# A two-layer transformer kernel: setup moved into the main program, first batch loaded first, rows fetched by two queues

## The chip, the cores and the metric

The kernel runs on one core of a Trainium2 chip. A core has TensorE (matmuls), VectorE (DVE in the rows), ScalarE (ACT), GpSimd (POOL) and SyncE (SP), each with its own list of instructions; they meet at semaphores. SP and ACT also issue DMA transfers, each in its own queue. The metric is the device time of one execution in microseconds, lower is better.

## What is computed

Four batches of 1024 tokens with 128 features pass four blocks, each with a layer norm ahead and a residual sum behind:

```python
x = x + attention0(layernorm(x))   # 16 heads of 8, causal, W_qkv and W_out
x = x + circulant(layernorm(x))    # fft, 128x128 product, ifft, bias
x = x + attention1(layernorm(x))   # 16 heads, one 8x8 weight for all heads, Wu and bu
x = x + experts(layernorm(x))      # 8 experts, top 2 by softmax of a small gate
```

## The kernel before

**Three programs, one after the other.** `setup` (lines 348 to 442) loads and prepares, `pipeline` (474 to 1042) does both attention layers and the circulant block, `experts` (1045 to 1174) the last block. Each is a block of instructions for all engines, and the engines wait for one another at its end.

**setup.** SP loads constants, weights and then all of x (2 MB, line 364), and raises every later semaphore by one, which is why waits of the pipeline are written `past(count)`, one more than the count. ScalarE's queue loads small weights. GpSimd clears buffers, among them the part of `k_rows` that is constant (line 388). VectorE repeats the 8x8 weights (`w8r`, 399), casts constants (401, 402) and moves transposed or multiplied weights out of PSUM (405 to 420), which TensorE makes (428 to 442).

**pipeline.** Attention is done in groups of four heads: 4 batches x 4 groups x 2 layers = 32 groups. What each engine does, and in which sequence, comes from one list, `ORDER`, that all engines walk. It is written out by hand in the strings `LINES`: a letter takes the next item of its stream.

- `r`: one of 18 "score" fills of a group: matmuls of queries and keys in a split bf16 form (line 602), two PSUM banks each, whose row maxima VectorE takes (930). These banks are a ring of two pairs.
- `H`: the "shift": the maxima are turned and written by DMA into rows of `q_rows` (549), so that the next matmuls subtract them.
- `u`: one of 36 "units" of a group: the scores again, transposed and shifted (634), then Exp on ScalarE (748) and for some the causal mask on GpSimd (857). A line of the strings holds the 36 units of one group, but for the first line, which has none.
- `v`, `c`, `O`: product with the values (657), its copy out of PSUM (767), its transpose and division (620, 978, 980).
- `w`: the DMA loads of a group's `q_rows` and `k_rows` (`load_rows`, nine transfers for each of two row tiles).
- `x`: the steps between, in the order of `steps_between`: for each batch the layer norm (`stats` 1001 to 1013, `rstd` 490 to 501, `norm` 1029), transposes `turn` (667), projections (677, 680), splitting of q and k into three bf16 parts, and their `store` in DRAM (521), from which `load_rows` reads. The first batch is split by ScalarE and VectorE (`part`, 810, 814, 1037, 1041), later ones by GpSimd (`split`, 896 to 905).

Layer norms ahead of layer 0 are on VectorE, most others on GpSimd. Transposes, projections and units share three PSUM banks in turn, and each is moved out by ScalarE (`evacuate`, 748), so a fourth waits until the first has been moved. The batch 0 stores of the first group's heads come first, on SP, then rows 0, then the stores of the other heads (538).

Of the kernel before, what the change touches and what calls it, by code (L numbers as in the profile page):

```python
# [93 lines left out]
def masks_before(n, pb):  # L94
# [23 lines left out]
    "uvruvuruuvcruuruvOuruuvruvuruuvcruuruvruuuvruruuuvruuuruvuuHuurruvuruw",  # L118
    "uvruvuruuvcruuruvOuruurxuvruvuruxruvcruuurvruuvruruuuvuruxxuuuvuHuruvuuuwrrvvx",
    "uruuvcruuuruOuruuvrurxuuvvruuuvcruxurxvruuvruruxxuruuvruxxuuuHvuruuuvuruuwrvvx",  # L120
    "uruuvcruuruOuuruvrxuruuvuruvruuxvcrxuruvruxxruuvruruxruuurvuxHuuvrxuruxxuruvruuxrxuw",
    "urvuvruruxxruurvcxrxuuOuuruvruuvxxruvruuuvcxrxruuuvurxuvHuuuvruruuuvruuruuruvuruw",
    "uruvuruuvruuruvcuruurvuOuruuvvruxruuruvcruxuruvHuuuvruruvuruuvruuurvuruuwr",
    "uuvruuvruuvcruuruvOuruuvvruuuvcruruuvruruuvuruuxxuuuvuHuruvuuurvuruuwr",
# [12 lines left out]
    "uruvuvruuruvcruuuxxuuuvuHuOuuuvxvruruuvcuruurxvuruvurxuuvruruxruuurvruuvruw",  # L137
    "uxruvruvuruuvcruuruvOuruuvuruvuruvcuuHuvruruvuruuuvruruuuvruruuurvuruuwr",
    "uuvuruvruuvcruuurvOuruuvruxuruvuruvcxHuuvruruvuruuuvruruuuvruruuurvuruuwr",
    "uuvuruvruuvcruuurvOuruuvruuxxuuuvuvcHuruuvxruuvruuuvrxuruuvruuuruuruvxruwr",  # L140
    "uxuvruvuruxruvcruuurvuOuruuvruuvruuuvcruruuvHuvruruuvruuuruvruuuruvruruuw",
    "uruvuvruuruvcuruurvuOuruuvruuvruuuvcruruuvHuvruruuvruuuruvruuuruvruruuw",
    "uruvuvruuruvcuruurvuOuruuvruxruuuvruvcruxuvHruuruvruuvruuuruvruruuurvuruuwr",
# [10 lines left out]
def preparation(layer, b):  # L154
# [7 lines left out]
    steps = normalisation(2 * layer, b) + [("bias", 2, b)] * layer  # L162
    (q0, q1), (k0, k1), (v0, v1) = halves(0), halves(1), halves(2)
# [184 lines left out]
def setup(nc, m, dram, sem, phase_semaphores):  # L348
    ident = m.const[:, C_ID:C_COS]
    cos, sin, nsin = (m.const[:, c:c + P] for c in (C_COS, C_SIN, C_NSIN))  # L350
    loaded, head_loaded, repeated, made, used, half, ready = (
        sem(n) for n in ("setup_loaded", "setup_w8_loaded", "setup_w8_repeated", "setup_psum", "setup_evacuated",
                         "setup_half", "setup_ready"))
    x_loaded, own = sem("setup_x_loaded"), sem("setup_memset")
    with nc.Block() as block:
        @block.sync
        def _(sp):
            sp.dma_start(m.const[:, :], dram["consts"]).then_inc(loaded, 16)
            sp.dma_start(m.raw[:, 0:3, :], dram["L0_attn_W_qkv"].rearrange("(n o) c -> o n c", o=P)).then_inc(loaded, 16)
            sp.dma_start(m.raw[:, 3, :], dram["L0_attn_W_out"]).then_inc(loaded, 16)  # L360
            sp.dma_start(m.raw[:, 4, :], dram["L1_attn_Wu"]).then_inc(loaded, 16)
            sp.dma_start(m.raw[:, 5, :], dram["L0_ffn_w_freq_real"]).then_inc(loaded, 16)
            sp.dma_start(m.raw[:, 6, :], dram["L0_ffn_w_freq_imag"]).then_inc(loaded, 16)
            sp.dma_start(m.x[:, :, :], dram["L0_attn_x"].rearrange("b (t p) d -> p (b t) d", p=P)).then_inc(x_loaded, 16)

            for semaphore in phase_semaphores:
                sp.sem_inc(semaphore, 1)
            sp.wait_ge(x_loaded, 16)

        @block.scalar  # L370
        def _(act):
            for n, name in enumerate(("L1_attn_Wq", "L1_attn_Wk", "L1_attn_Wv")):
                act.dma_start(m.w8[:, n, :], dram[name]).then_inc(head_loaded, 16)
            act.dma_start(m.bias_ffn[:, :], dram["L0_ffn_bias"].rearrange("(a d) -> a d", a=1).broadcast_to([P, D])).then_inc(m.late_loaded, 16)
            act.dma_start(m.bias_u[:, :], dram["L1_attn_bu"].rearrange("(a d) -> a d", a=1).broadcast_to([P, D])).then_inc(m.late_loaded, 16)
            act.dma_start(m.wg1[:, :], dram["L1_ffn_wg1"]).then_inc(m.late_loaded, 16)
            act.dma_start(m.bg1[:, :], dram["L1_ffn_bg1"].rearrange("(g a) -> g a", a=1)).then_inc(m.late_loaded, 16)
            act.dma_start(m.wg2[:, :], dram["L1_ffn_wg2"]).then_inc(m.late_loaded, 16)

        @block.gpsimd  # L380
        def _(pool):
            nc.gpsimd.memset(m.vg[:, :, :, :, :], 0.0).then_inc(own, 1)
# [42 lines left out]
        def _(pe):  # L425
            pe.wait_ge(loaded, 6 * 16)
            for n in range(4):
                last = nc.tensor.transpose(m.psum[:, 0, n * P:(n + 1) * P], m.raw[:, n, :], ident)
# [801 lines left out]
```

## Time and profile before

| | |
|---|---|
| median of 3 runs | 1220.77 us (1218.82 to 1221.8) |
| the profiled execution | 1220.89 us, span 1219.2 us |
| mean granted TensorE clock | 0.969 |
| TensorE busy | 1132.4 us (93%) |
| VectorE busy | 901.7 us (74%) |
| ScalarE busy | 770.1 us (63%) |
| GpSimd busy | 401.4 us (33%) |

The span runs from the first to the last instruction of the profile; the time of the execution is 1.7 us longer. Busy time of TensorE is modelled, and matmuls overlap. A granted clock of 1.00 is 2.4 GHz, one of 0.50 is 1.2 GHz, and a number between is a mean over time at either.

### The profile page before, as it was taken

The numbers are of one execution on the slowest core, as the hardware profiler recorded it, in microseconds if no ns is written. First come the engines' busy times: TensorE is split into PE (matmuls) and PEld (weight loads), VectorE is DVE, ScalarE is ACT, GpSimd is POOL, SyncE is SP. The second block draws the span as 40 slices with busy tenths as digits, with TensorE's granted clock in tenths as the row PEclk, the third lists the DMA queues.
The fourth block names the chain that finished last, engine by engine and source line by source line (L and its number), as shares of the span: only waits on it lengthen the run. The fifth ranks groups of instructions, "written<-read, shape, count | busy, mean of one in ns | idle before, by whom it ended". The sixth has DMA issues, their size and how long they took to land. (4 is left out here: it accounts for less than half of the span.)

```text
span 1219.2 us, 26837 instructions
## 1 busy us (share of the span) xinstructions
PE 1132.4 (93%) x9927; PEld 542.5 (44%) x9927; DVE 901.7 (74%) x1461; ACT 770.1 (63%) x1397; POOL 401.4 (33%) x667
## 2 busy tenths in 40 slices
PE   3479999999999999999999999999999799999997
PEld 2224343444344344433444344433342357777776
DVE  4698889998998999898899998898892253223223
ACT  1327678777888778787777787777777542322322
POOL 3143452555226462555356452142252000000000
PEclk9669999999999999899999999999998989999999
DMA  3230420112111011002111210011100000000000
GB/s 108 94 115 28 123 79 29 28 28 73 53 29 35 28 54 53 28 29 66 53 37 34 79 29 28 27 34 47 30 3 2 1 1 1 17 0 17 0 18 18
DMA packets 35336, 47.35 MB, mean 39 GB/s; under 512 B 8848, under 2 KB 15120, under 8 KB 35216
## 3 DMA queue, kind: packets, MB, share of 16 engines
q1 hardware_dynamic: 34640, 45.61, 13.1%
q8 instruction: 74, 1.21, 0.4%
q10 hardware_dynamic: 576, 0.15, 0.1%
q14 instruction: 46, 0.38, 0.1%
HBM read 30.53 MB, written 14.68 MB: 37 GB/s over the span
## 5 line engine op out<-in xcount | busy, mean ns | idle before, releaser
L748 ACT ACTIVATE probs<-psum 128x512 f32<-128x512 f32 x1152 | 614.3, 604 | 199.8 <-PE psum L634 197.6
L930 DVE TENSOR_REDUCE block_max<-psum 128x8 f32<-128x1024 f32 x576 | 672.3, 1218 | 70.4 <-PE psum L602 67.0
L634 PE MATMUL psum<-q_rows,k_rows 50*128 50x512 bf16 (+3 forms) x1536 | 325.1, 330 | 14.4 <-ACT probs L748 10.9
L657 PE MATMUL psum<-probs,vg 128*32 128x512 f32 (+3 forms) x3072 | 329.0, 504 | 7.4 <-POOL probs L857 4.4
L857 POOL TENSOR_SCALAR_AFFINE_SELECT probs<-probs 128x512 f32<-128x512 f32 (+1 forms) x320 | 173.9, 547 | 448.0 <-ACT probs L748 444.4
L602 PE MATMUL psum<-k_rows,q_rows 48*128 48x128 bf16 (+2 forms) x2560 | 261.4, 266 | 27.8 <-DMA k_rows<-k_split 17.7
L602 PEld LDWEIGHTS psum<-k_rows,q_rows 48*128 48x128 bf16 x2560 | 114.7, 95 | 180.6 <-DVE block_max L930 74.9
L634 PEld LDWEIGHTS psum<-q_rows,k_rows 50*128 50x128 bf16 x1536 | 105.1, 94 | 166.0 <-ACT probs L748 124.0
L1162 DVE SCALAR_TENSOR_TENSOR x<-psum,probs,x 128x128 f32 x256 | 69.1, 343 | 144.4 <-PE psum L1080 144.0
L1102 ACT ACTIVATE probs<-psum 128x1024 f32<-128x1024 f32 x64 | 65.5, 1024 | 151.5 <-PE psum L1067 151.5
L1080 PEld LDWEIGHTS psum<-w_out,probs 128*128 128x128 f32 x1024 | 119.2, 192 | 14.8 <-issue 12.9
L1080 PE MATMUL psum<-w_out,probs 128*128 128x128 f32 x1024 | 119.3, 275 | 0.0
L1067 PE MATMUL psum<-v,w_in 128*128 (+1 forms) x256 | 116.8, 600 | 0.6 <-PEq L504 0.6
L657 PEld LDWEIGHTS psum<-probs,vg 128*32 128x32 f32 x3072 | 63.0, 108 | 111.2 <-issue 70.1
L599 PE MATMUL psum<-mask 64*128 64x256 bf16 (+1 forms) x512 | 72.9, 334 | 0.8 <-DVE block_max L930 0.5
L875 POOL TENSOR_SCALAR xn<-x,mv,rstd 128x128 f32<-128x128 f32 x88 | 69.2, 798 | 0.3
L1067 PEld LDWEIGHTS psum<-v,w_in 128*128 128x128 f32 x256 | 46.9, 193 | 48.1 <-issue 47.9
L978 DVE RECIPROCAL rden<-psum 128x32 f32<-128x32 f32 x32 | 11.4, 357 | 53.1 <-PE psum L620 52.7
L599 PEld LDWEIGHTS psum<-mask 64*128 64x128 bf16 x512 | 20.5, 95 | 45.5 <-DVE block_max L930 24.1
L767 ACT ACTIVATE out_t<-psum 128x512 f32<-128x512 f32 x64 | 39.1, 611 | 0.1
L677 PE MATMUL psum<-xn_t,w 128*128 128x512 f32 x64 | 36.9, 668 | 0.3 <-ACT probs L748 0.2
L620 PE MATMUL psum<-const,out_t 128*128 128x128 f32 x256 | 34.9, 279 | 2.1 <-DVE block_max L930 1.2
(107 smaller groups left out, 617.4 us busy)
## 6 DMA issues: line engine op xcount, KB each, us to landing
k_rows<-k_split SPq DMA_DIRECT2D x384, 32.0 KB
q_rows<-q_split SPq DMA_DIRECT2D x64, 96.0 KB
q_split<-parts SPq DMA_DIRECT2D x21, 256.0 KB
k_split<-parts SPq DMA_DIRECT2D x21, 256.0 KB
q_rows<-q_split SPq DMA_DIRECT2D x64, 64.0 KB
q_rows<-q_split SPq DMA_DIRECT2D x64, 32.0 KB
out<-x SPq DMA_DIRECT2D x4, 512.0 KB, 3.2
q_rows<-shift_t SPq DMA_DIRECT2D x64, 8.0 KB
```

The costliest lines, as they stand in the source:

```text
L599: nc.tensor.matmul(blocks[:, :, upper], m.mask[tile, j, :], m.mask[tile, 2 + j, upper].unsqueeze(1).broadcast_to([ROW_TILE, 4, P - ROW_TIL ...
L602: done = nc.tensor.matmul(m.psum[:, bank, col:col + w], m.q_rows[rows_of(e, False), buf, pair, i * P:(i + 1) * P], m.k_rows[rows_of(e, Fal ...
L634: done = nc.tensor.matmul(m.psum[:, bank, col:col + w], m.k_rows[rows_of(e, True), buf, pair, kb * P:(kb + 1) * P], m.q_rows[rows_of(e, Tr ...
L657: done = nc.tensor.matmul(m.psum[32 * hh:32 * hh + 32, OUT_BANK, q0 % BANK:q0 % BANK + w], m.vg[:, n % 2, kb, hh, :], m.probs[:, (n * len( ...
L748: nc.scalar.activation(out, m.psum[rows, UNIT_AT[number % UNIT_DEPTH], 0:columns], function, **more).then_inc(bank_read, 1)
L857: nc.gpsimd.affine_select(out=tiles, in_=tiles, compare_op=ALU.is_ge, fill=0.0, base=0, pattern=pattern, channel_multiplier=-1).then_inc(m ...
L875: done = nc.gpsimd.tensor_scalar(m.xn[:, t, :], m.x[:, n, :], m.mv[:, n, 0:1], m.rstd[:, n:n + 1], ALU.subtract, ALU.mult)
L930: nc.vector.tensor_reduce(out, blocks, axis=AX.X, op=ALU.max).then_inc(ring_read, 1)
L1067: last = nc.tensor.matmul(m.psum[:, 2 * j + half, :], m.w_in[:, e % E, j * P:(j + 1) * P], m.xn_t_all[:, b + e // E, half * BANK:(half + 1 ...
L1080: last = nc.tensor.matmul(m.psum[:, bank + t // 4, (t % 4) * P:(t % 4 + 1) * P], m.hidden[:, 2 * (e % 2) + j, t * P:(t + 1) * P], m.w_out[ ...
L1102: nc.scalar.activation(m.hidden[:, 2 * (e % 2) + j, :], m.psum[:, 2 * j:2 * j + 2, :].rearrange("p a b -> p (a b)"), ACT.Gelu).then_inc(ge ...
L1162: last = nc.vector.scalar_tensor_tensor(xt[:, b, t, :], m.psum[:, bank + t // 4, (t % 4) * P:(t % 4 + 1) * P], top[:, b, t, e:e + 1], xt[: ...
```

## The change

`setup` is gone; its instructions stand at the heads or in the middle of the pipeline's instruction lists, without the wait of all engines between. x is loaded in two transfers, batch 0 ahead of everything else. The first weights go through PSUM bank 3 and a ScalarE copy, the others later through banks 4 to 6. Statistics and reciprocal deviations of batch 1 come before batch 0 is transposed, those of batch 2 before batch 1 is. Stores and row loads of batch 0's keys and of the second row tile move to ScalarE's queue. `LINES` is rewritten for the first groups and in many places behind (shown: the first four; 19 of the 33 lines are as some line of before, most of them at another place).

```diff
 LINES = (
-    "xxxxxxxxxxxxxxxxxxxxwwwxxxxxxrrxxxrxxrxxrxxrxxrxxxxxxxrrrrrrrrrrrrrHrrr",
-    "uuuruxxxxuruuruvuuuvvuuuvcuuuvuxuuvruruxuruvuruxruurvuruxruuvrxuruuxuwrvrvxxHvcrrxxxO",
-    "uurxrxuuruuruuvruxxruuvuvruuruvcxuruxurvurxxxxxuuvuururuvuuuuvuuuuvuuxuwvvrxrvrxcHxOxrxxr",
-    "uuuruxruxuruvruuruxruurxvuvruxxrxxuruvcuuruvxrxuuvrurxuuuvururuuvuHuuurruvuruw",
...
+    "xxxxxxxxxxxxxxxxxxxxxxwwwxxxxxxxxxxxxxxxxxrxxxxxxxrrrrrrrrrrrrrrrrrrrHrrr",
+    "uuuruxxuruuruvuuxvuvruruxuvcruuruvruxruurvuruxrxuruxxuruvHuxxruruvuruxxruuvruruxxruwr",
+    "uuvuruvruuvcruuurvuOuruuxxvvruuuvcxrurxuuvruuxxxxxuvururuvuuuuvuuuuvuuuwxvvvHxcrrxO",
+    "uruxruuruuruvxururuxruuvxuvruruxxuruvcurxxruuvruruxxxxxuxrurvuuuvxHuurruvuruuvruuuwr",
...
     steps = normalisation(2 * layer, b) + [("bias", 2, b)] * layer
+    if (layer, b) == (0, 0):
+        steps[4:4] = normalisation(0, 1)[:2]
+    elif layer == 0 and b < 3:
+        steps = steps[2:]
+        if b == 1:
+            steps[2:2] = normalisation(0, 2)[:2]
...
-def load_rows(m, engine, n, rows_loaded):
+def load_rows(m, engine, n, rows_loaded, tiles=(0, 1)):
...
-    for e in (0, 1):
+    for e in tiles:
...
+def first_stores(m, engine, which, heads, done):
+    dest = (m.q_dram, m.k_dram)[which][0].rearrange("h r d (b t) -> r b h d t", b=B)
+    for part in range(PARTS):
+        engine.dma_start(dest[part, 0, heads], m.parts[heads.start * DH:heads.stop * DH, which, part, :]).then_inc(done, 16)
...
         @block.sync
         def _(sp):
+            x = dram["L0_attn_x"].rearrange("b (t p) d -> p (b t) d", p=P)
+            sp.dma_start(m.x[:, 0:TT, :], x[:, 0:TT, :]).then_inc(m.x_first, 16)
+            sp.dma_start(m.const[:, :], dram["consts"]).then_inc(m.loaded, 16)
+            sp.dma_start(m.raw[:, 0:3, :], dram["L0_attn_W_qkv"].rearrange("(n o) c -> o n c", o=P)).then_inc(m.loaded, 16)
+            for semaphore in sems + m.later:
+                sp.sem_inc(semaphore, 1)
+            for n, name in ((3, "L0_attn_W_out"), (4, "L1_attn_Wu"), (5, "L0_ffn_w_freq_real"), (6, "L0_ffn_w_freq_imag")):
+                sp.dma_start(m.raw[:, n, :], dram[name]).then_inc(m.raw_loaded, 16)
+            sp.dma_start(m.x[:, TT:NT, :], x[:, TT:NT, :]).then_inc(m.x_rest, 16)
...
+                        if which == 0:
+
+                            sp.wait_ge(cast_made, past(3))
+                            sp.wait_ge(rest_made, past(3))
+                            first_stores(m, sp, 0, slice(0, GH), first_stored)
+                        continue
...
+                        sp.wait_ge(m.own, 5)
+                        load_rows(m, sp, 0, rows_loaded, (0,))
+                        first_stores(m, sp, 0, slice(GH, HEADS), stored)
...
+            first_weights()
             for item in ORDER:
...
                     project(item)
+                    if item[1:] == (0, 0, 2, 1):
+                        further_weights()
...
+            act.wait_ge(m.made, 1)
+            nc.scalar.activation(m.w[:, Q0:V0 + 1, :].rearrange("p a b -> p (a b)"), m.psum[:, OUT_BANK, 0:3 * P], ACT.Copy).then_inc(m.used, 1)
...
+                elif item == ("store", 0, 0, 1):
+
+                    act.wait_ge(cast_made, past(4))
+                    act.wait_ge(rest_made, past(4))
+                    first_stores(m, act, 1, slice(0, GH), first_stored)
+                elif item == ("rows", 0):
+
+                    act.wait_ge(first_stored, past(STORES))
+                    act.wait_ge(m.own, 5)
+                    load_rows(m, act, 0, rows_loaded, (1,))
+                    first_stores(m, act, 1, slice(GH, HEADS), stored)
...
+            def constants_cast():
+
+                dve.wait_ge(m.loaded, 2 * 16)
+                nc.vector.tensor_copy(m.ident_bf[:, :], ident).then_inc(m.cast, 1)
+                nc.vector.tensor_copy(m.mask[:, :, :].rearrange("p a b -> p (a b)"), m.const[:, C_MASK:C_HEAD]).then_inc(m.cast, 1)
+                dve.wait_ge(m.head_loaded, 3 * 16)
+                for n in range(3):
+                    nc.vector.tensor_copy(m.w8r[:, n, :, :], m.w8[:, n, :].unsqueeze(1).broadcast_to([DH, HEADS, DH])).then_inc(m.repeated, 1)
...
-                    if s > 0:
+                    if s == 0:
+
+                        dve.wait_ge(m.x_first if b == 0 else m.x_rest, 16)
+                    else:
...
                     done.then_inc(normalised, 1)
+                    if (s, b, half) == (0, 0, 1):
+                        constants_cast()
...
+                        if which == 1:
+                            further_weights()
```

`further_weights` on TensorE holds the three small matmuls, two transposes and six matmuls that setup had for the other weights, and on VectorE the seven moves out of PSUM. It stands behind the last projection of batch 0 on TensorE and behind the last part of batch 0's keys on VectorE.

## Rows read from the trace of the kernel before

**Rows 1.** Stages: busy us of each engine, granted TensorE clock, DMA share, GB/s.

```profile
17.70:50.30 32.60, 8.24 (x34) 5.21 (x34) 18.69 (x84) 9.85 (x13) 0.00 (x0) 0.76 0.12 38
82.00:145.00 63.00, 59.73 (x525) 23.32 (x526) 56.53 (x124) 45.60 (x87) 24.13 (x30) 0.94 0.30 84
145.00:900.00 755.00, 732.91 (x7344) 303.90 (x7347) 679.16 (x884) 584.42 (x1115) 333.04 (x579) 0.99 0.15 41
```

**Rows 2.** DMA issues of the start: size, us from issue to landing.

```profile
const<-in_consts SPq DMA_DIRECT2D x1, 552.0 KB, 3.8
...
x<-in_L_attn_x SPq DMA_DIRECT2D x1, 0.5 KB, 13.1
```

**Rows 3.** Timeline of the first 26 us: start, duration, instruction, [idle before].

```profile
3.03 0.45 ACTq L376 DMA_DIRECT2D wg<-in_L_ffn_wg  x1
3.13 7.10 POOL L388 MEMSET k_rows<- 32x4096 f32 x2
...
3.84 0.93 SPq L364 DMA_DIRECT2D x<-in_L_attn_x  x1
...
10.67 0.42 DVE L402 CAST mask<-const 128x512 bf16<-128x512 f32 x1
...
17.75 1.65 DVE L1001 BATCH_NORM_STATS2 stats<-x 128x6 f32<-128x128 f32 x8 [0.53 <-PEq L355]
...
20.10 0.17 DVE L1011 TENSOR_SCALAR newton<-mv 128x8 f32<-128x8 f32 x1
...
23.23 2.14 DVE L1029 TENSOR_SCALAR xn<-x,mv,rstd 128x128 f32<-128x128 f32 x8
```

**Rows 4.** Line 399 alone: shortest, median and longest of three, in ns.

```profile
L399 DVE COPY w8r<-w x3: 1407/1482/3606, 5.2 to 6.7; 8x128 f32<-8x128 f32 x3
```

**Rows 5.** Timeline around 87 us.

```profile
87.26 0.64 POOL L857 TENSOR_SCALAR_AFFINE_SELECT probs<-probs 128x512 f32<-128x512 f32 x1 [0.83 <-ACT probs L748]
87.34 0.58 DVE L490 TENSOR_SCALAR newton<-newton 128x8 f32<-128x8 f32 x1
```

**Rows 6.** Timeline from 26 to 54 us.

```profile
26.33 4.52 PE L677 MATMUL psum<-xn_t,w 128*128 128x512 f32 x8
...
32.46 2.36 DVE L1037 TENSOR_TENSOR qk<-qk,parts 128x1024 f32<-128x1024 f32 x2 [7.09 <-ACT parts L810]
...
34.81 2.36 DVE L1041 TENSOR_TENSOR parts<-qk,parts 128x1024 bf16<-128x1024 f32 x2
35.82 1.07 ACT L748 ACTIVATE v<-psum 128x512 f32<-128x512 f32 x2
...
38.35 1.84 SPq L521 DMA_DIRECT2D k_split<-parts  x3
...
42.22 1.10 SPq L467 DMA_DIRECT2D q_rows<-q_split  x3
...
46.50 2.00 SPq L471 DMA_DIRECT2D k_rows<-k_split  x6
...
50.29 1.03 PE L602 MATMUL psum<-k_rows,q_rows 48*128 48x512 bf16 x4 [17.66 <-DMA k_rows<-k_split]
...
51.41 2.29 SPq L538 DMA_DIRECT2D k_split<-parts  x3
...
53.13 2.08 PE L677 MATMUL psum<-xn_t,w 128*128 128x512 f32 x2
```

**Rows 7.** Two stretches behind the idle time, columns as in rows 1.

```profile
50.30:55.50 5.20, 5.20 (x16) 2.30 (x16) 2.35 (x2) 1.40 (x3) 0.00 (x0) 0.50 0.66 209
55.50:63.00 7.50, 7.50 (x56) 3.93 (x56) 6.13 (x5) 3.38 (x6) 5.29 (x4) 1.00 0.34 105
```

**Rows 8.** Timeline from 63 to 82 us.

```profile
63.01 10.28 DVE L930 TENSOR_REDUCE block_max<-psum 128x8 f32<-128x1024 f32 x9 [0.52 <-PE psum L602]
...
75.90 0.42 DVE L938 TENSOR_REDUCE low<-block_max 128x32 f32<-128x256 f32 x1
...
81.94 1.03 PE L634 MATMUL psum<-q_rows,k_rows 50*128 50x512 bf16 x3 [0.32 <-DMA q_rows<-shift_t]
```

More of the change, by code:

```diff
@@ L463, in load_rows @@
                     for d in (m.q_dram[layer], m.k_dram[layer]))
-    for e in (0, 1):
+    for e in tiles:
         for first, count in ((0, 3), (3, 2), (5, 1)):
@@ L511, in _ @@
                     if (layer, b) == (0, 0):
[L513 to L517 removed]
+                        if which == 0:
[3 more added lines that the diff above has]
+                        continue
+                    sp.wait_ge(split_done, past(at_split(layer, b, which) + 1))
                     dest = (m.q_dram, m.k_dram)[which][layer].rearrange("h r d (b t) -> r b h d t", b=B)
[L519 removed]
                     for part in range(PARTS):
[L521 removed]
+                        sp.dma_start(dest[part, b], m.parts[:, which, part, :]).then_inc(stored, 16)
                 elif kind == "rows":
@@ L532, in _ @@
                         sp.wait_ge(bank_filled, past(UNIT_AT_ORDER["unit", n - GROUPS, NU - 1] + 1))
-                    load_rows(m, sp, n, rows_loaded)
                     if n == 0:
-                        for which, dram_parts in enumerate((m.q_dram[0], m.k_dram[0])):
-                            dest = dram_parts.rearrange("h r d (b t) -> r b h d t", b=B)
-                            for part in range(PARTS):
-                                sp.dma_start(dest[part, 0, GH:HEADS], m.parts[GH * DH:P, which, part, :]).then_inc(stored, 16)
+                        sp.wait_ge(m.own, 5)
+                        load_rows(m, sp, 0, rows_loaded, (0,))
+                        first_stores(m, sp, 0, slice(GH, HEADS), stored)
+                    else:
+                        load_rows(m, sp, n, rows_loaded)
                     if n == GROUPS:
@@ L581, in scores @@
                 buf = n % GROUPS
+                if (n, s) == (0, 0):
+                    pe.wait_ge(m.cast, 2)
                 if s == 0:
@@ L825, in _ @@
         def _(pool):
+            nc.gpsimd.memset(m.vg[:, :, :, :, :], 0.0).then_inc(m.own, 1)
+            nc.gpsimd.memset(m.block_max[:, :, :, :, :, :, :].rearrange("p n h e a i k -> p (n h e a i k)"), -3.0e38).then_inc(m.own, 1)
+            k_words = m.k_rows[:, :, :, :].rearrange("p g h t -> p (g h t)").bitcast(FP32)
+            pool.wait_ge(m.own, 2)
+            for e in (0, 1):
+                nc.gpsimd.memset(k_words[ROW_TILE * e + 32:ROW_TILE * (e + 1), :], TWO_ONES).then_inc(m.own, 1)
+            pool.wait_ge(m.own, 4)
+            nc.gpsimd.memset(m.vg[:, :, :, :, DH:DH + 1], 1.0).then_inc(m.own, 1)
+            pool.wait_ge(m.own, 5)
             v = m.v[:, :, :].rearrange("p (b t) (g h d) -> p b g t h d", b=B, g=GROUPS, h=GH)
@@ L958, in _ @@
                 if kind == "score":
+                    if item[1:] == (0, 0):
+                        dve.wait_ge(m.own, 5)
                     take_scores(item, bank)
@@ L1186, in preln_two_layers @@
         moe = [sem(f"moe_{name}") for name in EXPERT_SEMAPHORES]
-        setup(nc, m, dram, sem, flow + moe)
+        m.later = moe
+        m.x_first = sem("setup_x_first")
+        m.x_rest = sem("setup_x_rest")
+        m.loaded = sem("setup_loaded")
+        m.raw_loaded = sem("setup_raw_loaded")
+        m.head_loaded = sem("setup_head_loaded")
+        m.repeated = sem("setup_repeated")
+        m.made = sem("setup_made")
+        m.used = sem("setup_used")
+        m.cast = sem("setup_cast")
+        m.own = sem("setup_own")
         pipeline(nc, m, dram, flow)
```

155 lines of the change are left out of this document (57 added, 98 removed).

## The prediction

> **What bounds the kernel now.** I read the whole span by stages first [rows 1], then the start instruction by instruction. From 145 to 900 us TensorE is busy 732.9 of 755 us at granted clock 0.99, VectorE 679, ScalarE 584: in the long middle TensorE sets the pace, and 22.1 us of it are idle. From 82 to 145 TensorE is busy 59.7 of 63, so here too little is lost but clock (0.94). From 17.7 to 50.3 it is busy 8.2 of 32.6 us. So the run is a start in which TensorE waits, then a stretch that it fills. Whatever brings its first "unit" matmul (81.94 us [rows 8]) forward should come off the end, as long as the stretch behind it keeps its length.
>
> What fills the start: x lands 13.1 us after its issue at 3.84, so at 16.94 [rows 2, 3]. The barrier ends and statistics begin at 17.75, normalising at 23.23 and ends 25.37 [rows 3]. Projections and splitting end at 37.17, stores are issued until 40.19, the loads of group 0's rows start at 42.22, and the first score matmul starts at 50.29 [rows 6]. Eighteen score reductions of VectorE later group 0's maxima are reduced at 75.90, and the first unit follows at 81.94 [rows 8].
>
> **The change, part by part.** All times are of the profiled execution.
>
> *x first, no barrier.* The first batch of x is now first in SP's queue: 512 KB. The nearest row is the 552 KB of constants, first in the queue before: issued at 0.80, landed 3.8 us later, at 4.6 [rows 2]. x has shorter pieces, so I take 5.2 (bounds 4.6 and 7.5, twice the time). Statistics and aggregation took 20.10 - 17.75 = 2.35 us, so the first small TENSOR_SCALAR comes due at 7.55.
>
> *GpSimd in the way.* The memsets stay at the start; the two of k_rows run from 3.13 to 10.23 [rows 3]. Before, VectorE was waiting for the weights meanwhile. What it did then was the copies of w8r, and these took 1.41, 1.48 and 3.61 us [rows 4] for 8 x 128 elements, the last ending at 10.3, just after the memset, although a cast of 128 x 512 takes 0.42 [rows 3]. Later a TENSOR_SCALAR of 128 x 8 at 87.34 took 0.58 us, against 0.17 for one like it [rows 3], and ended at 87.92, when the GpSimd operation of 87.26 to 87.90 did [rows 5]. So the chain of TENSOR_SCALARs will be held until 10.23. The Trainium skill says this as a rule, on the page "SBUF — State Buffer", section "Who interferes with whom": a VectorE copy or tensor_scalar in a two-port mode and a GpSimd instruction lock one port pair against each other, and the later one waits for the whole of the earlier. It speaks against this change, since it takes back part of the early load; the two rows agree with it. From 10.23, the rest of the chain as before (25.37 - 20.10 = 5.27) ends the normalising at 15.5; without the hold it would be 5.2 + 7.62 = 12.8.
>
> *Constants and the weights.* The constants and W_qkv now queue behind 512 KB. If that delays them by as much as 552 KB took in all, they land at 4.6 + 3.8 = 8.4; with three transposes and one ScalarE copy they are ready by about 11. The first projection came 26.33 - 25.37 = 0.96 after the normalising [rows 3, 6], so it comes at 16.5. They cost nothing; if later than that they push everything by the excess. Behind the normalising VectorE casts the constants and repeats w8: 0.42 for the larger cast, some 1.3 us in all (estimate from that row, five copies).
>
> *Statistics of batch 1 brought forward.* VectorE must now finish them before the splitting (parts). They wait for the other 1.5 MB of x. SP issues that after 36 semaphore increments, which no row prices, and four weights, at some 0.45 each if like the small load on ScalarE's queue [rows 3]. Before, all bytes had landed at 16.94; the order of bytes changes, not their sum. I take 16 (bounds 14.5 and 18.5). After the casts VectorE is free at 16.8, statistics and reciprocal take 23.23 - 17.75 = 5.48, to 22.3. The parts could start 32.46 - 25.37 = 7.09 after the normalising, at 22.6. So this move is just hidden; x landing at 18.5 costs 1.4. The parts end 4.71 later [rows 6]: **27.3** instead of 37.17 (bounds 26.2 without the hold and 28.7).
>
> *Stores and rows by two queues.* K's three stores move to ScalarE's queue, 1.84 us from 27.4; the rows start 42.22 - 40.19 = 2.03 after them, at 31.3. Of 18 row loads (42.22 to 48.5, 0.35 each) ScalarE issues nine, 3.1 us, then three more stores, 2.29 [rows 6]: it is held until **36.7**. ScalarE's own issues cost 0.45 where shown [rows 3], like SP's. The rows land at 31.3 + 3.1 + 1.8 = 36.2. On SP the remaining Q stores shorten alike, and rows 1 and 2 come earlier than before; they are needed only some 20 us later.
>
> *What is queued behind.* In the new order all of batch 1's transposes and projections but the last stand before the first score on TensorE, and their evacuations, with those of V of batch 0, stand on ScalarE behind its DMA issues. So the rows are not what the first score waits for. From 36.7: two V evacuations and one of the transposes at 0.54 [rows 6], 38.3; then q0, q1, k0, k1, v0. One 128 x 512 projection takes 1.13 at clock 1.00 (4.52 for four) and 2.08 after an idle stretch [rows 6]; from 50.30 the clock was 0.50 for 5.2 us of steady work and then 1.00 [rows 7]. So two at 2.08 and three at 1.1: first score at **45.8** (43.8 all fast, 48.7 all slow).
>
> *Other weights.* VectorE's seven operations lay between 10.67 and 17.75 before [rows 3], so they and TensorE's between them take 7.1 us at most, until 34.4 now; batch 1's normalising (2.14) ends by 36.5 and batch 2's statistics by 42. All this is covered by the same wait; beyond 36.7 the normalising would delay the transposes one for one.
>
> *Scores.* Before, projections stood between the first seven scores: the seventh ended at 63.01. From there eleven took 12.89, or 1.17 each. Eighteen now take 21.1, 0.5 is what VectorE waits for the first of them (as before 63.01), and some 0.8 goes to the one projection left in between (part of 1.1 to 2.08): 45.8 + 22.4 = 68.2 [rows 8], and the first unit comes 81.94 - 75.90 = 6.04 later: **74.2**, against 81.94. Gain 7.7 us, bounds 3.4 (x late by 1.4, low clock 2.9) and 10.8 (no hold 1.1, high clock 2.0).
>
> *The order behind.* The same matmuls are there, so I charge only idle time. From 82 to 145 TensorE idled 3.3 us [rows 1], mostly where a group's shift came last in its line. The new line puts shift 1 before twelve units of group 0, and VectorE no longer has batch 2's statistics there. I take 1.5 gained; bounds 3.3 gained and 3.3 lost. From 145 on the lines are rearranged, and without a trace of them I take nothing, bounds a few us either way.
>
> **Sum:** 7.7 + 1.5 = 9.2. The profiled execution took 1220.89 us (span 1219.2), 0.1 above the median 1220.77: 1220.9 - 9.2 = **1211.7**.
>
> **Rivals.**
>
> *VectorE's lead counts, not TensorE's.* VectorE is 56.5 of 63 us busy behind the start [rows 1], and TensorE's idle moments there may all be its waits. The seventh score then ends at 45.8 + 0.8 + 0.5 + 8.2 = 55.3 against 63.01, and 5.48 of statistics lie before it: 13 ahead, 1208. Against it: TensorE is busier in that stretch.
>
> *ScalarE's issues eat the gain.* Fifteen DMA issues now hold ScalarE on the chain. If each costs 0.6 us more there than on SP, the 9.2 are gone and the time is 1221, no change. The rows of small issues speak against it; none shows a store or a row load on that queue.
>
> *The new order stalls in the middle (slower).* One mechanism: scores run further ahead of the units there, so TensorE more often waits at a full ring or for an evacuation. Idle there is 22.1 us now. It eats the gain when it grows by 9.2 us, and the kernel is slower beyond +0.3% when it grows by 13. If it doubled, 1220.9 - 9.2 + 22.1 = 1233.8. For it: TensorE is at 97% and any misplaced wait counts. Against it: 19 of the 33 lines are lines of before, moved by up to five places.
>
> *No hold by GpSimd.* Parts end at 26.2, 1210.6; inside the forecast's own range.
>
> **How the numbers follow.** Forecast 0.60 (with the no-hold variant), VectorE's lead 0.20, ScalarE's issues 0.09, stalls 0.07, a still larger gain 0.04. The forecast's best bounds give 1220.9 - 10.8 - 3.3 = 1206.8; the start at its worst bound with nothing from the order gives 1217.5; the first rival, 1208, lies between. With a little for the middle stretch the range is 1205 to 1218, which leaves out the slower cases, most of no change and the larger gain. 0.3% is 3.7 us, about what a measurement of this kernel can tell from no change: faster below 1217.1 in 0.83, within it 0.10, slower 0.07.
>
> **What would show it.** Statistics begin near 5 us, the TENSOR_SCALARs behind them stand until about 10.2, normalising ends near 15.5; parts end near 27; ScalarE issues until 37; first score near 46, first unit near 74; then TensorE's idle time from there to the end about as before. The prediction fails if the rest of x lands past 20, if ScalarE's issues take far over 0.35 to 0.76 us, or if the stretch from the first unit to the end is more than 4 us longer or shorter than its 1137 us now.

## The result and the profile after

The change takes 1206.44 us (median of 6, 1204.44 to 1210.68) against 1218.88 us for the kernel before on the same chip (6, 1217.97 to 1221.8): ratio 0.9897, interval 0.9883 to 0.9912, so 12.4 us less. Forecast were 9.2 less, 1211.7. The profiled execution took 1204.83 us (span 1203.1) at a mean granted clock of 0.976, against 0.969 in the profile before.

First the start, instruction by instruction.

Chosen rows from the timeline of the changed kernel, 3 to 75 us (start, duration, instruction, [idle before]); the timelines further down are chosen rows too:

```profile
3.13 7.06 POOL L815 MEMSET k_rows<- 32x4096 f32 x2
4.90 1.65 DVE L1026 BATCH_NORM_STATS2 stats<-x 128x6 f32<-128x128 f32 x8 [4.90 <-DMA x<-in_L_attn_x]
7.26 2.96 DVE L1036 TENSOR_SCALAR newton<-mv 128x8 f32<-128x8 f32 x1
13.22 2.14 DVE L1054 TENSOR_SCALAR xn<-x,mv,rstd 128x128 f32<-128x128 f32 x8
16.32 5.44 PE L606 MATMUL psum<-xn_t,w 128*128 128x512 f32 x8
16.52 1.65 DVE L1026 BATCH_NORM_STATS2 stats<-x 128x6 f32<-128x128 f32 x8 [0.29 <-DMA x<-in_L_attn_x]
23.37 2.36 DVE L1064 TENSOR_TENSOR qk<-qk,parts 128x1024 f32<-128x1024 f32 x2 [1.41 <-ACT parts L783]
25.72 2.36 DVE L1068 TENSOR_TENSOR parts<-qk,parts 128x1024 bf16<-128x1024 f32 x2
28.17 2.00 ACTq L386 DMA_DIRECT2D k_split<-parts  x3
33.03 1.13 ACTq L376 DMA_DIRECT2D q_rows<-q_split  x3
34.18 2.13 ACTq L380 DMA_DIRECT2D k_rows<-k_split  x6
36.35 2.72 ACTq L386 DMA_DIRECT2D k_split<-parts  x3
39.12 1.09 ACT L710 ACTIVATE v<-psum 128x512 f32<-128x512 f32 x2 [12.30 <-issue]
39.86 1.09 PE L596 MATMUL psum<-const,xn 128*128 128x128 f32 x4 [6.65 <-ACT v L710]
40.75 5.20 PE L606 MATMUL psum<-xn_t,w 128*128 128x512 f32 x8
46.77 0.39 PE L531 MATMUL psum<-k_rows,q_rows 48*128 48x512 bf16 x2
68.60 0.42 DVE L933 TENSOR_REDUCE low<-block_max 128x32 f32<-128x256 f32 x1
74.66 1.03 PE L563 MATMUL psum<-q_rows,k_rows 50*128 50x512 bf16 x3 [0.34 <-DMA q_rows<-shift_t]
```

Read it as a chain. Statistics begin at 4.90 instead of 17.75 [rows 3]. The first TENSOR_SCALAR takes 2.96 us, where one like it took 0.17 before [rows 3]: it ends at 10.22, when the GpSimd memset does (10.19). So of 12.85 us gained at the load, 10.0 are left when normalising begins (13.22 against 23.23), 9.1 at the splitting (23.37 against 32.46 [rows 6]), and then ScalarE spends 28.17 to 39.07 issuing DMAs and waiting for them. Its next work, two copies of V out of PSUM, starts at 39.12 after 12.30 us without work. The second half of batch 1's transposes (L596) has waited 6.65 us for them at 39.86, the projections run at 40.75 behind it, and the first score matmul comes at 46.77, only 3.5 before the old 50.29 [rows 6]. Some is made up again, since just one projection is left between the scores: the first unit stands at 74.66 instead of 81.94 [rows 8].

The w8r copies, 1.4 to 3.6 us each beside the memsets before [rows 4], now run at 15.7, behind them; durations are shortest, median, longest in ns:

```profile
L952 DVE COPY w8r<-w x3: 207/207/208, 15.7 to 16.0; 8x128 f32<-8x128 f32 x3
```

From the first unit on, by the windows of the changed kernel (columns as in [rows 1]):

```profile
75.00:140.00 65.00, 58.90 (x536) 23.48 (x532) 56.52 (x96) 45.93 (x87) 24.33 (x30) 0.95 0.30 83
140.00:900.00 760.00, 739.44 (x7444) 308.63 (x7445) 687.48 (x887) 593.03 (x1131) 343.77 (x599) 1.00 0.15 41
```

TensorE idles 6.1 us of the first 65 (3.3 of 63 before), and 20.6 of the next 760 (22.1 of 755 before [rows 1]). So the early start is not eaten in the middle. How far ahead the changed kernel is can be followed by the first unit instruction of each group, read in both timelines (us; the experts block follows the last group):

| | group 0 | group 3 | group 8 | group 24 | group 31 | experts | end |
|---|---|---|---|---|---|---|---|
| before | 81.94 | 174.27 | 310.93 | 751.83 | 932.52 | 986.93 | 1219.18 |
| after | 74.66 | 167.68 | 300.71 | 744.11 | 921.41 | 970.87 | 1203.13 |
| ahead | 7.28 | 6.59 | 10.22 | 7.72 | 11.11 | 16.06 | 16.05 |

The row "ahead" also says where the new order gains, and it is not where the forecast put it. From group 0 to 3, the stretch right behind the start, the lead shrinks by 0.7 us. From 3 to 8 it grows by 3.6 and from 24 to 31 by 3.4; between them, from 8 to 24, it shrinks by 2.5, although there the kernel before spent 10.2 us at half clock and the changed one 6.8. The second profile of the change (f1 below) has the same steps: 92.7, 133.0 and 177.3 us from 0 to 3, 3 to 8 and 24 to 31, against 92.3, 136.7 and 180.7 before.

The last step was no part of the forecast. From group 31 to the experts both kernels do the same matmuls, yet the one takes 54.41 us and the other 49.46. The granted clock differs. Windows before (columns as above):

```profile
932.52:940.00 7.48, 7.45 (x45) 1.61 (x45) 0.00 (x0) 5.57 (x11) 3.08 (x6) 0.54 0.01 2
...
975.00:980.00 5.00, 5.00 (x26) 2.71 (x25) 1.30 (x6) 2.35 (x4) 0.00 (x0) 0.79 0.00 0
980.00:987.00 7.00, 5.60 (x24) 2.62 (x23) 0.07 (x1) 1.91 (x5) 0.00 (x0) 0.76 0.00 0
```

and after:

```profile
921.41:930.00 8.59, 8.15 (x76) 3.06 (x76) 0.78 (x2) 7.06 (x15) 4.15 (x8) 1.00 0.01 2
...
960.00:965.00 5.00, 4.95 (x31) 3.05 (x30) 2.93 (x13) 2.67 (x5) 0.00 (x0) 1.00 0.01 2
965.00:971.00 6.00, 4.61 (x28) 2.98 (x28) 0.12 (x1) 1.97 (x5) 0.00 (x0) 1.00 0.01 3
```

Before, TensorE was at 1.2 GHz for 13.7 of these 54.4 us; after, at 2.4 throughout. This differs between executions of one kernel: f2 and g0 below, one kernel twice, spent 3.6 and 13.7 us of this stretch at half clock. Whether the change also makes it rarer is open (see the part on the prediction). To take the clock out of comparisons I added up, over windows of 10 us from 15 us behind the first unit to group 31, the time at half clock, 2 x (1 - granted clock) x length, and took half of it off the stretch. That assumes that work at 1.2 GHz takes twice its time; it is an estimate, and called "corrected" below. Before: 850.58 with 10.2 us at half clock, corrected 845.5. After: 846.75 with 6.8, corrected 843.4. So the new order is worth some 2.1 us behind the first unit. (The 15 us left out hold 5.5 to 8.0 us at half clock in every profile; with them taken out too it is 1.7.)

### The profile page after: what moved, and what is told of

The parts are those of the page before. It is cut to its first block and busy times, and to the rows that moved or that the text cites. A ratio compares the mean times of both kernels' runs of the same rounds, so it can differ in the third digit from the quotient of the medians.

```text
span 1203.1 us, 26830 instructions
## 1 busy us (share of the span) xinstructions
PE 1122.7 (93%) x9927; PEld 542.4 (45%) x9927; DVE 901.9 (75%) x1461; ACT 770.6 (64%) x1398; POOL 401.8 (33%) x667
## 5 line engine op out<-in xcount | busy, mean ns | idle before, releaser
L531 PE MATMUL psum<-k_rows,q_rows 48*128 48x128 bf16 (+2 forms) x2560 | 262.1, 266 | 12.5 <-DVE block_max L925 10.5
L528 PE MATMUL psum<-mask 64*128 64x512 bf16 (+1 forms) x512 | 73.7, 335 | 1.6 <-DVE block_max L925 1.3
L606 PE MATMUL psum<-xn_t,w 128*128 128x512 f32 x64 | 37.6, 690 | 0.0
L596 PE MATMUL psum<-const,xn 128*128 128x128 f32 x128 | 22.6, 304 | 15.1 <-ACT v L710 6.6
```

Source lines behind the costliest of these rows:

```text
L528: nc.tensor.matmul(blocks[:, :, upper], m.mask[tile, j, :], m.mask[tile, 2 + j, upper].unsqueeze(1).broadcast_to([ROW_TILE, 4, P - ROW_TIL ...
L531: done = nc.tensor.matmul(m.psum[:, bank, col:col + w], m.q_rows[rows_of(e, False), buf, pair, i * P:(i + 1) * P], m.k_rows[rows_of(e, Fal ...
```

## The experiments

All medians are of full kernels; "first unit" and "stretch" (first unit to group 31) are from one profiled execution each. The ratios are to executions of the kernel before on the same chip: median 1219.06 (17) beside e1 to e4, 1218.63 (11) beside f1 to f4, 1219.9 (11) beside g0 to g2.

| run | median us | ratio (interval) | first unit | stretch | at half clock | corrected |
|---|---|---|---|---|---|---|
| before | 1218.88 | 1 | 81.94 | 850.58 | 10.2 | 845.5 |
| the change | 1206.44 | 0.9897 (0.9883 to 0.9912) | 74.66 | 846.75 | 6.8 | 843.4 |
| f1_change_again | 1205.78 | 0.9891 (0.9875 to 0.9908) | 73.95 | 846.44 | 6.8 | 843.0 |
| f3_order_alone | 1212.15 | 0.9943 (0.9925 to 0.9961) | 80.08 | 845.13 | 3.4 | 843.4 |
| e1_order_before | 1208.69 | 0.991 (0.9896 to 0.9925) | 72.66 | 847.52 | 3.4 | 845.8 |
| e2_one_queue | 1204.67 | 0.9876 (0.9859 to 0.9893) | 68.93 | 847.61 | 6.8 | 844.2 |
| e3_memset_late | 1207.73 | 0.9894 (0.9879 to 0.991) | 73.55 | 849.48 | 13.8 | 842.6 |
| e4_x_whole | 1215.32 | 0.9974 (0.9955 to 0.9992) | 83.11 | 844.89 | 3.4 | 843.2 |
| f4_filled_end | 1204.98 | 0.9903 (0.9872 to 0.9934) | 73.30 | 845.18 | 3.4 | 843.5 |
| f2_best_start | 1201.11 | 0.9855 (0.984 to 0.9869) | 67.57 | 846.91 | 6.8 | 843.5 |
| g0_best_again | 1201.65 | 0.9849 (0.9832 to 0.9866) | 67.96 | 847.19 | 6.8 | 843.8 |
| g1_best_filled | 1200.78 | 0.9846 (0.9829 to 0.9863) | 67.64 | 845.15 | 3.4 | 843.4 |
| g2_best_order_before | 1205.36 | 0.9892 (0.9872 to 0.9911) | 70.75 | 848.57 | 3.4 | 846.9 |

### The change once more

> The changed kernel itself, to compare with the others of this call. Both theories: about 12 us (1.0%) below the kernel before, between 1204 and 1211, the higher of its times with the lower mean clock.

No edit. The median, 1205.78, agrees with the first. Three profiles hold this very start (the change, f1 and, with an edit only far behind, f4): the first unit stands at 74.66, 73.95 and 73.30. What differs is when TensorE becomes faster. Among batch 0's projections the weight loads of L606 start 0.85 us apart until 19.83, 18.97 and 18.13, and 0.43 apart behind; so four projections take 5.44, 5.00 and 4.57 us, and the splitting starts at 23.37, 22.93 and 22.50. Batch 1's four start under a clock of 0.50 and take 5.20, 5.02 and 4.83. So differences under 1.4 us at the first unit count only where several profiles agree.

### The two halves, each alone

The order alone, on the old setup with its barrier:

```diff
 (in the kernel before)
-LINES = ( lines of before )
+LINES = ( lines of the change )
     steps = normalisation(2 * layer, b) + [("bias", 2, b)] * layer
+    if (layer, b) == (0, 0):
+        steps[4:4] = normalisation(0, 1)[:2]
+    elif layer == 0 and b < 3:
...
```

> The kernel before with only the order of the change: its strings, and statistics of batches 1 and 2 brought forward; the setup program with its barrier, x loaded whole and one queue stay. Theory (the order gives what it gave behind the first unit, and the scores without projections between them): statistics of batch 1 are hidden before the parts, first score near 50.3 as before, first unit near 78.3 instead of 81.9, and from there to the experts some 4 us less than before with the same clock: 7 us below the kernel before. Rival (the order gives only the 2 us by which the change beats the run with the order of before): 2 us below the kernel before, with the first unit at 80 or later.

Its timeline:

```profile
50.87 0.61 PE L608 MATMUL psum<-k_rows,q_rows 48*128 48x512 bf16 x2 [5.05 <-DMA k_rows<-k_split]
...
80.08 1.03 PE L640 MATMUL psum<-q_rows,k_rows 50*128 50x512 bf16 x3 [0.31 <-DMA q_rows<-shift_t]
```

6.5 us less than before: 1.9 at the first unit, 2.1 behind it (843.4 against 845.5), and the remaining 2.5 are no more than the clock falls vary; they are not explained further. Here batch 1's projections run while the rows are fetched: the first score still waits 5.05 us for the rows, so they cost nothing.

The start alone, by giving the changed kernel the old lines and steps (the edit above, the other way):

> The change with the order of before: setup in the one program, x first and two queues stay, but the strings of the order and the list of steps are those of before (statistics of batches 1 and 2 back at their old places). Theory (the start sets the gain, the order behind it little): the rows land at about 38 us, as in the changed kernel, and the old order has no projection of batch 1 ahead of the first score, so the first score starts near 38 instead of 46.8 and, with 31.65 us from there to the first unit as before the change, the first unit near 70 instead of 74.7. Then the time is 12 us below the kernel before, as much as the change itself, or a few us more gain. Rival (the rewritten order is what brings the gain beyond the 7.3 us of the start): the first unit near 70 but the stretch behind it 4 us longer than in the changed kernel, or the first unit no earlier than 74; then the gain is at most 8 us.

Its timeline:

```profile
33.79 2.00 SPq L374 DMA_DIRECT2D k_rows<-k_split  x6
33.88 2.06 ACTq L374 DMA_DIRECT2D k_rows<-k_split  x6
...
40.84 1.04 PE L525 MATMUL psum<-k_rows,q_rows 48*128 48x512 bf16 x4 [10.81 <-DMA k_rows<-k_split]
...
72.66 1.03 PE L557 MATMUL psum<-q_rows,k_rows 50*128 50x512 bf16 x3 [0.32 <-DMA q_rows<-shift_t]
```

10.4 us less than before, 9.28 of them at the first unit; the stretch behind is that of before (845.8). So the start is the larger half. With the new start the old order reaches its first unit 0.6 to 2.0 us earlier than the new one, where on the old start the new order was 1.9 ahead. The first score waits for the rows themselves here, and they come at 40.84, 2.8 later than I expected, though the last load is issued by 35.94.

### One queue for stores and rows

```diff
 (SP)
+                        else:
+                            sp.wait_ge(cast_made, past(4))
+                            sp.wait_ge(rest_made, past(4))
+                            first_stores(m, sp, 1, slice(0, GH), first_stored)
...
-                        load_rows(m, sp, 0, rows_loaded, (0,))
-                        first_stores(m, sp, 0, slice(GH, HEADS), stored)
+                        load_rows(m, sp, 0, rows_loaded)
+                        for which in (0, 1):
+                            first_stores(m, sp, which, slice(GH, HEADS), stored)
 (ScalarE)
-                elif item == ("store", 0, 0, 1):
-                elif item == ("rows", 0):
...
```

> The change with all stores and row loads of batch 0 on SP's queue again. Theory (the first score waits for the projections of batch 1, and these for ScalarE, which its DMA issues hold until 39.1 us): SP's stores end near 31, rows start near 33, 18 loads of 0.35 us and 1.8 to land give 41.2; ScalarE is free, so the projections of batch 1 are over by 40; first score near 41.2 instead of 46.8, first unit near 69, time 5.5 us below the changed kernel. Rival (two queues help by what they save in issues): the first score comes 3 us or more later, near 50, and the time is 3 us above the changed kernel.

Its timeline:

```profile
26.25 1.06 ACT L715 ACTIVATE v<-psum 128x512 f32<-128x512 f32 x2
28.75 1.84 SPq L386 DMA_DIRECT2D k_split<-parts  x3
...
33.37 4.98 PE L611 MATMUL psum<-xn_t,w 128*128 128x512 f32 x8
...
36.93 2.01 SPq L380 DMA_DIRECT2D k_rows<-k_split  x6
...
41.07 0.39 PE L536 MATMUL psum<-k_rows,q_rows 48*128 48x512 bf16 x2 [1.83 <-DMA k_rows<-k_split]
...
68.93 1.03 PE L568 MATMUL psum<-q_rows,k_rows 50*128 50x512 bf16 x3 [0.31 <-DMA q_rows<-shift_t]
```

ScalarE copies V at 26.25 instead of 39.12, the projections start 7.4 earlier, and the first score is back to waiting for its rows, at 41.07. The first unit comes 4.4 to 5.7 us before those of the three profiles above: the second queue cost that much instead of saving anything. The median fell by only 1.8, but this profile spent 13.7 us of its last stretch at half clock (54.80 us against 49.46), and in the executions themselves the mean clock ran from 0.974 (1201.85) to 0.969 (1207.81); the median alone would not have settled it, f2 and g0 below do.

Nor did the second queue fetch rows sooner. From the first row load's issue to the first score it took 8.19 us in e1 with two queues (32.65 to 40.84), 8.42 here with one (32.65 to 41.07) and 8.48 in g2 below (30.36 to 38.84), although with two the issues ended three microseconds earlier. The Trainium skill says in "DMA: Bandwidth & Descriptors", section "Issuing engines are not separate DMA queues", that engines that issue share the same 16 DMA engines, so that a second one saves issue time and no transfer time. These three rows agree; what they add is that the issue time saved on SP was paid on ScalarE. One thing is not apart here: in e1 six stores of the other heads, 192 KB each, are issued from 35.83 on, while the rows are still landing, and in e2 only from 38.98 on. Whether rows from two queues would land sooner without these stores no run shows.

### The memsets out of the way

```diff
             pool.wait_ge(m.own, 2)
+            pool.wait_ge(rstd_ready, past(2))
```

> The change with GpSimd's memset of the k_rows waiting until the reciprocal deviations of batch 1 are made. Theory (the memset holds VectorE's small TENSOR_SCALARs until 10.2 us): the one that took 2.96 us takes 0.17, normalising ends near 12.5 instead of 15.4; then the statistics of batch 1, which wait for the rest of x at 16.5, set the start of the parts: 22.0 instead of 23.4, first unit 1.4 us earlier, time about 1.4 us below the changed kernel. Rival (the held instruction waits for something else, the landing of a transfer or a semaphore): it still ends near 10.2 and nothing moves.

Its timeline:

```profile
7.39 0.17 DVE L1037 TENSOR_SCALAR newton<-mv 128x8 f32<-128x8 f32 x1
10.50 2.14 DVE L1055 TENSOR_SCALAR xn<-x,mv,rstd 128x128 f32<-128x128 f32 x8
16.37 1.65 DVE L1027 BATCH_NORM_STATS2 stats<-x 128x6 f32<-128x128 f32 x8 [2.86 <-DMA x<-in_L_attn_x]
21.72 2.35 DVE L1065 TENSOR_TENSOR qk<-qk,parts 128x1024 f32<-128x1024 f32 x2
21.92 7.06 POOL L816 MEMSET k_rows<- 32x4096 f32 x2 [18.86 <-DVE rstd L416]
```

The TENSOR_SCALAR takes 0.17 us again and normalising starts 2.72 earlier: the hold is shown. But only 1.65 of it reaches the splitting, since batch 1's statistics now wait 2.86 us for the rest of x, which lands at 16.4 either way. The memsets beside the splitting cost it nothing (2.35 against 2.36 us). The first unit, 73.55, lies within those of the unedited start, so here the gain isn't resolved, and the median isn't better; with one queue it is 1.0 to 1.4 us at the first unit (67.57, 67.96, 67.64 against 68.93 in e2's one profile).

### x in one piece, behind the weights

```diff
-            sp.dma_start(m.x[:, 0:TT, :], x[:, 0:TT, :]).then_inc(m.x_first, 16)
...
-            sp.dma_start(m.x[:, TT:NT, :], x[:, TT:NT, :]).then_inc(m.x_rest, 16)
+            sp.dma_start(m.x[:, :, :], x).then_inc(m.x_rest, 16)
...
-                        dve.wait_ge(m.x_first if b == 0 else m.x_rest, 16)
+                        dve.wait_ge(m.x_rest, 16)
```

> The change with x loaded whole and last, as before, so that the statistics of batch 0 wait for all of it. Theory (loading batch 0 first is worth 9 to 10 us, the missing barrier less than 1): statistics start near 17 instead of 4.9, no TENSOR_SCALAR is held, normalising ends near 24.6 instead of 15.4, all behind it 9.2 us later, first unit near 84, time 9 us above the changed kernel, some 3 us below the kernel before. Rival (the barrier was what cost): the time stays within 4 us of the changed kernel.

Its timeline:

```profile
17.49 1.64 DVE L1025 BATCH_NORM_STATS2 stats<-x 128x6 f32<-128x128 f32 x8 [17.49 <-DMA x<-in_L_attn_x]
22.96 2.14 DVE L1053 TENSOR_SCALAR xn<-x,mv,rstd 128x128 f32<-128x128 f32 x8
...
83.11 1.03 PE L562 MATMUL psum<-q_rows,k_rows 50*128 50x512 bf16 x3 [0.32 <-DMA q_rows<-shift_t]
```

1215.32, 8.9 more than the change; the first unit comes 8.45 later, so microseconds lost at the start come out at the end about one for one. Without the barrier but with x whole, statistics begin at 17.49 against 17.75, 0.3 us sooner. (x lands at 17.49 here and at 16.94 before, since it is issued at 5.84 instead of 3.84; the wait for the barrier behind its landing was 0.8.) So what gains is the order of the bytes. Its first unit is even 1.2 later than that of before.

### Is it the pauses that lower the clock?

The clock falls in the last stretch, where layer norms leave TensorE idle now and then. Two kernels fill such pauses with 18 matmuls of 512 columns whose result is not used, f4 in the change and g1 in the best start of below:

```diff
+            def fill(count):
+                for _ in range(count):
+                    nc.tensor.matmul(m.psum[:, OUT_BANK, :], m.ident_bf[:, :], m.mask[:, :, :].rearrange("p a b -> p (a b)"),
+                                     start=True, stop=True)
+            FILLED = (("turn_att", 1, 3, 0), ("mix", 1, 3), ("logits", 1), ("turn", 3, 3, 0), ("logits", 2), ("logits", 3))
...
+                if item in FILLED:
+                    fill(3)
```

> The change with 18 matmuls more (bf16, 128x128 by 128x512, into the bank of the attention output, read by nobody) on TensorE in the last stretch before the experts, three each ahead of six instructions that wait there. Theory (the fall of the clock to 1.2 GHz between 955 and 990 us follows the waits of that stretch, and is most of the difference between runs of one kernel): granted clock 1.00 there, the stretch from the last group's first unit to the experts takes 49.5 to 51 us in the profile, and no run is as slow as the slowest of the changed kernel: median 1.5 to 2.5 us lower. Rival (the fall has nothing to do with that idle time): the clock falls as often, and the matmuls add 1 to 4 us.

> The same with the 18 matmuls that fill TensorE's waits ahead of the experts. Theory (the fall of the clock in that stretch follows those waits): no fall there, the stretch from the last group's first unit to the experts near 50, median 1 to 2.5 us below the run without them. Rival (what the fill saves it costs, or the clock falls elsewhere): the medians agree within 1 us.

f4's profile shows no fall there (50.45 us, clock 1.00), but its six executions run from 1202.33 to 1216.33, the longest at a mean clock of 0.964, and f1's profile, unfilled, lost only 3.6 us at half clock there. f4 says nothing. In g1 the clock fell all the same, by its windows

```profile
900.00:910.00 10.00, 8.82 (x60) 2.06 (x57) 2.16 (x5) 8.36 (x17) 0.41 (x1) 1.00 0.01 3
910.00:920.00 10.00, 9.18 (x60) 2.14 (x60) 0.00 (x0) 7.58 (x15) 4.12 (x8) 0.64 0.01 2
920.00:930.00 10.00, 9.24 (x67) 3.56 (x63) 0.78 (x2) 6.70 (x15) 1.28 (x2) 0.85 0.00 0
```

but that does not refute the fillers: the fall begins at 912.8, and the first fillers run 32 us later:

```profile
944.37 0.59 PE L656 MATMUL psum<-mask,ident_bf 128*128 128x512 bf16 x2
```

From 923 to 967, where they lie, the clock stayed at 1.00. g1's median, 1200.78, is within 1 us of g0's. So neither run settles whether pauses bring the clock down. What the profiles do show is that TensorE's work just ahead of this place is not enough to tell. g0 and f2 are one kernel; here are its 10 us ahead of the first unit of group 31 and the 10 us behind it, first in g0, then in f2:

```profile
905.18:915.18 10.00, 8.40 (x62) 1.99 (x55) 0.22 (x1) 7.93 (x16) 1.45 (x3) 1.00 0.01 3
915.18:925.18 10.00, 10.00 (x56) 3.32 (x57) 0.12 (x1) 5.54 (x11) 3.71 (x7) 0.51 0.01 2
...
904.51:914.51 10.00, 8.40 (x63) 2.00 (x55) 0.22 (x1) 7.93 (x16) 1.45 (x3) 1.00 0.01 3
914.51:924.51 10.00, 9.52 (x86) 3.40 (x86) 0.78 (x2) 8.47 (x18) 4.35 (x8) 1.00 0.01 2
```

In all thirteen profiles TensorE is busy 8.4 of the 10 us ahead of this unit. In five (before, e1, e2, g0, g1) the clock falls within 0.2 us of it, in the other eight it stays at 1.00. What decides it stays open.

### Best start, and the order on it

f2 is e2 and e3 together; g0 is the same kernel once more.

> The change with one queue (SP) for the stores and rows of batch 0 and the late memset of k_rows, both together. Theory (their gains at the start add, since the chain is the parts, then SP's stores and rows): parts end near 26.4, rows land and first score near 39.5, first unit near 67.3, 7.4 us before that of the changed kernel; the time is 6 us below it with the same mean clock, near 1200.5. Rival (the start no longer sets the end, as the 1.8 us that one queue gained for 5.7 us at the first unit may say): the first unit near 67.3 all the same, but the time within 3 us of the changed kernel.

> The kernel with one queue for batch 0 and the late memset once more. Both theories: first unit near 67.6, time 17 us (1.4 to 1.5%) below the kernel before.

The timeline of f2:

```profile
39.71 0.39 PE L536 MATMUL psum<-k_rows,q_rows 48*128 48x512 bf16 x2 [0.64 <-DMA k_rows<-k_split]
...
67.57 1.03 PE L568 MATMUL psum<-q_rows,k_rows 50*128 50x512 bf16 x3 [0.32 <-DMA q_rows<-shift_t]
```

1201.11 and 1201.65, ratios 0.9855 and 0.9849: it beats both kernels, 17.5 and 18.3 us below the kernel before, 4.7 below f1, the change beside it. The first unit, 5.3 to 7.1 earlier than in the change's profiles, accounts for it. Last, g2 gives this start the old order (the memsets then wait for the w8r copies):

> One queue for batch 0, with the strings and the list of steps of before; the memset of k_rows waits for the repeated weights instead, since the statistics of batch 1 come later there. Theory (with ScalarE free the rewritten order no longer costs at the first unit, and behind it it saves 2.4 us): parts end near 25, first score near 38.3, first unit near 70 (31.65 us later, as before the change), the stretch from there to the last group's first unit 845.7 us plus what a lower clock costs, time about 4 to 5 us above the kernel with the new order. Rival (the order is worth nothing or harms): the time is equal or lower.

Its timeline:

```profile
38.84 1.04 PE L530 MATMUL psum<-k_rows,q_rows 48*128 48x512 bf16 x4 [10.89 <-DMA k_rows<-k_split]
...
70.75 1.03 PE L562 MATMUL psum<-q_rows,k_rows 50*128 50x512 bf16 x3 [0.32 <-DMA q_rows<-shift_t]
```

It takes 1205.36, 3.7 more than g0 beside it. The profiles show 2.8 at the first unit and 3.1 in the corrected stretch; that the medians differ by less I put down to the clock (g0's profile 0.970, g2's 0.975), which isn't shown. Here the first score comes 0.9 earlier than in f2, but the projections of batch 1 then lie between the scores. So the new order gains at the first unit when ScalarE is free (2.8 here, 1.9 in f3) and loses 0.6 to 2.0 when the second queue holds ScalarE.

## Why the prediction was right

The time fell inside the range, 5.3 us below the value forecast; 2.0 of these are the base, since the forecast started from 1220.9 and six executions of the kernel before have a median of 1218.88. The chain through the start was right in its mechanism and close in size. The gain behind it was right in size but not in place, which is luck, and the clock was missing. One of the prediction's own signs of failing came true: the stretch from the first unit to the end was to stay within 4 us of 1137, and it took 1128.5 in the change's profile and 1129.7 in f1. Of the 8.8 us less, 5.0 lie behind group 31, where the clock differs (54.41 against 49.46); of the other 3.8 the estimate above gives 2.1 to the order and 1.7 to the clock.

By its steps:

- **x first.** 5.2 forecast for x, 4.90 measured. Right; e4 shows that it carries the gain.
- **GpSimd in the way.** TENSOR_SCALARs held until 10.23, measured 10.22; normalising ended at 15.36 for 15.5. e3 shows the cause. The variant without hold was forecast at 1.1 us, measured 1.0 to 1.4 with one queue.
- **Constants, weights, other weights** cost nothing: the projections came at 16.32 for 16.5, 0.96 behind the normalising. The other weights were done at 31.0, where at most 34.4 was allowed. The rest of x landed at 16.5 for 16.
- **The parts** started at 23.37 for 22.6 and ended at 28.08 for 27.3. The step lacked that four projections take 5.44 us here, not the 4.52 of before [rows 6], since TensorE becomes faster 3.5 us into them instead of some 2; in three profiles the parts started between 22.50 and 23.37.
- **Stores and rows.** ScalarE was held until 39.07, forecast 36.7: 2.4 mis-sized. Of it 0.8 came with the parts, the wait between stores and rows was 2.86 (30.17 to 33.03) instead of 2.03, and stores cost 2.00 and 2.72 for three on ScalarE's queue where I put 1.84 and 2.29 from SP's. (That is not a dearer queue: SP's own three stores of Q took 2.09 and 2.83 in the same trace.) That the rows land at 36.2 was wrong by more (40.84 in e1), unseen, because what is queued behind ScalarE set the first score, as the step said.
- **First score** 46.77, 46.09, 45.40 in three profiles, forecast 45.8. I had two projections at the low clock and three at the high one after 38.3; they began later and ran together faster, so two misses cancelled in part; that the sum fits so well is luck. The 1.13 per projection was no figure of the high clock either: in the 4.52 us it comes from, weight loads start 0.85 us apart at first and 0.43 apart from 28.5 on, so that at the high clock one follows the other in 0.86.
- **Scores to first unit** 27.9 us (46.77 to 74.66), forecast 28.4. Gain at the first unit 7.3 to 8.6, forecast 7.7.
- **The order behind** 1.5 forecast, 2.0 to 2.5 in the corrected stretch of three profiles. The place was wrong: the 1.5 were to come from less idle time between 82 and 145 us, but TensorE's idle time in the 65 us behind the first unit grew from 3.3 to 6.1 us and the lead shrank by 0.7 up to group 3. What gained lies from group 3 to 8 and from 24 to 31, where the forecast took nothing.

Start and order so make 9.4, 10.5 and 10.6 of the 12.4 us in the three profiles. The other two to three go with the clock: before shows 0.972 or 0.973 in 15 of the 17 executions beside e1 to e4 (1217.3 to 1220.33), while the change showed 0.976 in three of six (1204.44 to 1205.78). Its two executions at 0.972 took 1207.1 and 1209.06, some 11 below those of before. The two executions of before at 0.977 took 1215.9 and 1215.95, again some 11 above those of the change at 0.976. The forecast had no term for this. It is not only chance of the execution: of the 39 executions of before beside the experiments 2 had a mean clock of 0.974 or more, of the twelve of the change and f1 8 had. Why the changed kernel keeps more of its clock is not shown.

The rivals. *VectorE's lead counts*: its time, 1208, was nearer than mine, but not by its mechanism: at group 3 the changed kernel is 6.59 us ahead, not 13, and TensorE's idle time behind the start grew from 3.3 to 6.1 us. *ScalarE's issues eat the gain*: the right place, a quarter of the price. It needed 9.2 us beyond the forecast's own hold, and ScalarE was held 2.4 us longer than forecast. e2 puts the whole hold at 4.4 to 5.7 us at the first unit, of which the forecast already carried most. *Stalls in the middle*: TensorE's idle time there fell from 22.1 to 20.6.

## What to carry to other kernels

Where the first engine waits for data and the bounding engine is full afterwards, follow the early microseconds from engine to engine to the first instruction of the full stretch: of 12.85 us gained at the load 7.3 to 8.6 arrived, and each loss had an instruction beside it in the timeline. An engine that computes on the path is a poor place for a second DMA queue, since all that stands behind the issues waits for them, and here the transfers did not come sooner. When a median moves by a few microseconds, compare executions with the same mean clock, or stretches with the clock taken out, before an edit is given credit.

## What the runs showed of the hardware

- The granted clock falls to 1.2 GHz in some executions of a kernel and not in others, behind the same work: at the first unit of group 31 in g0 and not in f2, with TensorE busy 8.40 of the 10 us ahead in both. The time at half clock in a last stretch was 0 to 13.7 us, and the stretch took 49.46 us or 54.8 for the same matmuls. Executions of one kernel spread over 1.4 us (e1, 1207.62 to 1209.05) to 14.7 (e4, 1210.68 to 1225.37), the 17 of before over 3.3.
- One TENSOR_SCALAR of 128 x 8 took 2.96 us beside a GpSimd memset and 0.17 without it, the w8r copies 1.4 to 3.6 and 0.21; a TENSOR_TENSOR with two inputs took 2.35 beside the memset and 2.36 without.
- Three stores took 1.84 to 2.84 us to issue on SP's queue and 2.00 to 2.79 on ScalarE's, nine row loads 3.1 and 3.26: no dearer queue is shown.
